# Who scales x by dt in a Mamba-2 block: ScalarE from PSUM, or GpSimd from SBUF

## The chip, the cores and the metric

The kernel runs on one core of a Trainium2 chip. The metric is the device time of one launch in microseconds, lower is better. The engines are named as the profile names them: PE (TensorE, matrix products), DVE (VectorE), ACT (ScalarE), POOL (GpSimd), SP (SyncE, which here only issues DMAs).

## The reference

Three blocks follow one another on x of 2 x 2048 tokens and 256 features: a routed feed-forward block, a Mamba-2 block, and the feed-forward block again.

```python
x = x + 0.5 * ffn(layernorm(x))
x = x + mamba2(layernorm(x))
x = x + 0.5 * ffn(layernorm(x))
```

Only the middle block changes. With 8 heads of 64 columns and a state of 64:

```python
z, xBC, dt = split(x @ W_in)
dt = softplus(dt + dt_bias)
xBC = silu(causal_conv4(xBC) + conv_b)        # gives x_ssm (512), B (64), C (64)
dA = exp(dt * A)
s = s * dA + (dt * x_ssm) outer B             # per token, per head
y = s . C + D * x_ssm
y = rmsnorm(y * silu(z)) * norm_weight
out = y @ W_out
```

## The kernel before

`mamba_block` cuts the 4096 tokens into 32 chunks of 128. Inside a chunk the recurrence is written as matrix products: `within(i)` (L1259) multiplies the masked decays `ex` by `xdt`, which is x times dt; `from_state(i)` (L1244) adds what the state before the chunk gives; `to_state(i)` (L1267) makes the new state from `xt`, which by then holds x times dt times the decay to the chunk's end.

Each engine has its own program, a loop over slots `s`, with a fixed order of steps in the slot and semaphore waits between engines. An engine never goes past a step that waits. Several chunks are in flight: in slot s chunk s is finished, chunk s+1 is prepared, chunks s+8 to s+10 are loaded and normalised. Four chunks share a group for the projection and the convolution, so the work of a slot also depends on s modulo 4 (tables `PROJECTED` and `TAPPED`, L835 and L836): blocks of 128 channels are projected in slots with remainder 3, 0 and 1, and convolved in slots with remainder 0, 1 and 2. Projection ends with group 7, so slots 27 to 31 have neither.

The steps round the change, for chunk s+1 unless said otherwise:

- PE `turn_xc` (L1297) transposes x into the PSUM bank `pT`. `turn_y(s)` (L1327) later writes the transposed y of chunk s into the same bank, so it must wait until x has been read from it.
- ACT `copy_x` (L1156) copies `pT` into `xt` in SBUF. Then ACT makes, in this order, `first_taps` of the first block of the slot where there is one, `decay(s+1, 1)` (four exponentials, L1171), `turn_x(s+9)` (L1126), `square(s)` (L1174), `copy_yT(s)` (L1178), `tanh` of convolved blocks and `first_taps` of a late block.
- POOL `scale_x` (L1062) makes three products of 128x512 from `xt`: `xdt` (L1068), `xD` (L1069) and, in place, `xt` (L1070). POOL's other steps in a slot are `decay_state`, `add_skip`, `gate_y`, `powers` and `add_tap`.
- PE after `turn_xc`: project the first block, `sums(s+1, 1)`, `turn_x(s+9)`, `turn_y(s)`, `project_z(s+2)`, project a late block, `turn_x2(s-2)`, and then, in the next slot, `from_state`, `project_dt` (which waits for DVE's `split_x`, L1491), `score`, `out_product`, `sums`, `within`, `to_state`.

The three waits that the change touches stand in these lines:

```python
pool.wait_ge(y_ready.sem, y_ready.done(i - 1))      # L1067, xdt is free again
pe.wait_ge(xdt_done.sem, xdt_done.done(i))          # L1260, within(i)
pe.wait_ge(xt_done.sem, xt_done.done(i + 1))        # L1330, turn_y(i)
```

Of the kernel before, what the change touches and what calls it, by code (L numbers as in the profile page):

```python
# [10 lines left out]
ALU = mybir.AluOpType  # L11
ACT = mybir.ActivationFunctionType
# [812 lines left out]
H = 8  # L825
HD = DIN // H
CONV = 4
NB = (DIN + 2 * NS) // P
GC = 4
# [11 lines left out]
def mamba_block(nc, c, keep, x, ys_d, w_in, conv_w, conv_b, dt_bias, a_log, d_skip, norm_w, w_out, x2, xn_d, batches):  # L841
# [6 lines left out]
    with ExitStack() as ctx:  # L848
# [5 lines left out]
        def step(name, unit=1):  # L854
# [25 lines left out]
        dts = sb("dts", [P, 3, NR, GC * H])  # L880
# [6 lines left out]
        xt, xdt, xD = (sb(n, [P, DIN]) for n in ("xt", "xdt", "xD"))  # L887
# [7 lines left out]
        DTR, DPOS, DABS, DU, DS, DS2, DQ, DT, DA, NCUM, ECUM, DEC, DECDT, ETOT = range(NR)  # L895

        pT, pP, small, pE, pY, pS, pZ, pO = (ctx.enter_context(nc.psum_tensor(f"bank{n}", [P, 512], F32)) for n in range(8))
# [13 lines left out]
        add1, add2, stats, aggr, stats2, aggr2, var_done, pow_done, nmr_done, norm_done, norm2_done = (  # L911
            step(n) for n in ("add1", "add2", "stats", "aggr", "stats2", "aggr2", "var", "pow", "nmr", "norm", "norm2"))
        xT_ready, xT_hi, xT_lo, z_ready, tz_done, sz_done, dt_ready, dt_added, x2T_ready, x2T_copied, logit_ready, logit_copied = (
            step(n) for n in ("xT", "xT_hi", "xT_lo", "z", "tz", "sz", "dt", "dt_added", "x2T", "x2T_copied", "logit", "logit_copied"))
        soft, exp_u, a_done, al_done, rest_done, cum_ready, cum_copied, exps, dec_in, dec_out, decdt, halo = (
            step(n) for n in ("soft", "exp_u", "a", "al", "rest", "cum", "cum_copied", "exps", "dec_in", "dec_out", "decdt", "halo"))
        p_ready, raw_done, tap0, tap_act, tap1, taps, tb_done, xc_done = (
            step(n) for n in ("p", "raw", "tap0", "tap_act", "tap1", "taps", "tb", "xc"))
# [4 lines left out]
        yT_ready, yT_copied, o_ready, xo_done = (step(n) for n in ("yT", "yT_copied", "o", "xo"))  # L923

        def row(G, n, k=0, chunks=GC):

            return dts[:, G % 3, n, k * H:(k + chunks) * H]

        def per_head(ap, width, parts=P):

            return ap.rearrange("p (h a) -> p h a", a=1).to_broadcast([parts, ap.shape[1], width])

        def by_head(ap, heads=H):
            return ap.rearrange("p (h d) -> p h d", h=heads)
# [4 lines left out]
        def live(i):  # L939
            return 0 <= i < T  # L940
# [75 lines left out]
        @block.gpsimd  # L1016
        def _(pool):
            chain = Chain(pool, consts)
            pool.memset(ident_bf[:, :], 0.0)
            pool.memset(future[:, :, :], 0.0)  # L1020
            pool.memset(S[:, :], 0.0)
            pool.memset(raw[:, :, 0:CONV - 1], 0.0)
            chain.link(pool.memset(pick[:, :], 0.0))
            for part in range(3):
                chain.link(pool.affine_select(out=pick[:, :], in_=pick[:, :], compare_op=ALU.not_equal, fill=1.0,
                                              base=-part * CH, pattern=[[-1, CH]], channel_multiplier=1))
            chain.link(pool.affine_select(out=ident_bf[:, :], in_=ident_bf[:, :], compare_op=ALU.not_equal, fill=1.0,
                                          base=0, pattern=[[-1, P]], channel_multiplier=1))
            chain.link(pool.affine_select(out=future[:, :, :], in_=future[:, :, :], compare_op=ALU.is_ge, fill=-1e30,
                                          base=0, pattern=[[0, GC], [1, P]], channel_multiplier=-1))  # L1030
            for s in (pow_done, xdt_done, xw_done, s1_done, td_done, yv_done, tap1):
                s.open(pool)

            def powers(s):

                q = s % 2
                pool.wait_ge(var_done.sem, var_done.done(at(s)))
                if live(s + 7):
                    pool.wait_ge(norm_done.sem, norm_done.done(s + 7))
                if live(s - 4):  # L1040
                    pool.wait_ge(norm2_done.sem, norm2_done.done(s - 4))
                if live(s - 3):
                    pool.wait_ge(xo_done.sem, xo_done.done(s - 3))
                pool.tensor_tensor(rstd[:, q, :], ve[:, q, :], c["neghalf"][:, 0:3], ALU.pow).then_inc(pow_done.sem, 1)  # L1044

            def decay_state(i):
                pool.wait_ge(S_done.sem, S_done.done(i - 1))
                pool.wait_ge(exps.sem, exps.done(i // GC))
                pool.wait_ge(i_ready.sem, i_ready.done(i))
                pool.tensor_tensor(by_head(S[:, :]), by_head(S[:, :]), per_head(dts[0:NS, i // GC % 3, ETOT, (i % GC) * H:(i % GC + 1) * H], HD, NS), ALU.mult).then_inc(s1_done.sem, 1)  # L1050

            def add_skip(i):
                pool.wait_ge(xw_done.sem, xw_done.done(i))
                pool.wait_ge(t1_done.sem, t1_done.done(i))
                pool.tensor_tensor(yv[:, :], yv[:, :], xD[:, :], ALU.add).then_inc(td_done.sem, 1)

            def gate_y(i):
                pool.wait_ge(sz_done.sem, sz_done.done(i))
                pool.wait_ge(t2_done.sem, t2_done.done(i))
                pool.tensor_tensor(yv[:, :], yv[:, :], sz[:, i % 2, :], ALU.mult).then_inc(yv_done.sem, 1)  # L1060

            def scale_x(i):  # L1062

                G, k = i // GC, i % GC
                pool.wait_ge(decdt.sem, decdt.done(G))
                pool.wait_ge(xt_done.sem, xt_done.done(i))
                pool.wait_ge(y_ready.sem, y_ready.done(i - 1))  # L1067
                pool.tensor_tensor(by_head(xdt[:, :]), by_head(xt[:, :]), per_head(row(G, DT, k, 1), HD), ALU.mult).then_inc(xdt_done.sem, 1)  # L1068
                pool.tensor_tensor(by_head(xD[:, :]), by_head(xt[:, :]), per_head(heads[:, 2, :], HD), ALU.mult)  # L1069
                pool.tensor_tensor(by_head(xt[:, :]), by_head(xt[:, :]), per_head(row(G, DECDT, k, 1), HD), ALU.mult).then_inc(xw_done.sem, 1)  # L1070

            def add_tap(G, m):
                b, j = ORDER[m], pooled(G, m)
                pool.wait_ge(tap_act.sem, tap_act.done(j))
                pool.tensor_tensor(acc[:, G % 2, b, :], acc[:, G % 2, b, :], tap[:, :], ALU.add).then_inc(tap1.sem, 1)  # L1075

            for s in SLOTS:
                if live(s):
                    if not ends(s):
                        decay_state(s)  # L1080
                    add_skip(s)
                    gate_y(s)
                if live(s + 1):
                    scale_x(s + 1)
                if rooted(s + 1):
                    powers(s + 1)
                for G, m in blocks(s, PROJECTED):
                    if m in BY_POOL:
                        add_tap(G, m)

        @block.scalar
        def _(act):
            for s in (al_done, norm_done, norm2_done, x2T_copied, logit_copied, xT_hi, tz_done, exp_u, exps, dec_out, raw_done, tap0, tap_act, tb_done,
                      xt_done, bt_done, ex0_done, ex_done, sq_done, yT_copied):
                s.open(act)
            act.dma_start(wst[:, :, :], w_in.rearrange("(k p) n -> p k n", p=P)).then_inc(in_loaded, 16)
            act.dma_start(wo[:, :, :], w_out.rearrange("(k p) n -> p k n", p=P)).then_inc(loads, 16)
# [58 lines left out]
            def copy_x(i):  # L1156
                act.wait_ge(turned.sem, turned.done(i))
                act.wait_ge(s_ready.sem, s_ready.done(i - 1))
                act.activation(xt[:, :], pT[:, :], ACT.Copy).then_inc(xt_done.sem, 1)

            def decay(i, half):

                G, k = i // GC, i % GC
                ready, done = ((e0_ready, ex0_done), (e1_ready, ex_done))[half]
                if half == 0:
                    act.wait_ge(cum_copied.sem, cum_copied.done(G))
                    act.wait_ge(y_ready.sem, y_ready.done(i - 2))
                act.wait_ge(ready.sem, ready.done(i))
                for n in range(GC):
                    h = half * GC + n  # L1170
                    last = act.activation(ex[:, i % 2, h, :], pE[:, n * P:(n + 1) * P], ACT.Exp, bias=dts[:, G % 3, NCUM, k * H + h:k * H + h + 1])  # L1171
                last.then_inc(done.sem, 1)
# [10 lines left out]
            for s in SLOTS:  # L1183
                first, late = blocks(s, PROJECTED)[:1], blocks(s, PROJECTED)[1:]
                G, G2 = cum_group(s), soft_group(s)
# [32 lines left out]
                    first_taps(*B)  # L1218
                if live(s + 1):
                    decay(s + 1, 1)  # L1220
                if live(s + 9):
                    turn_x(s + 9)
                if live(s):
# [8 lines left out]
        def _(pe):  # L1232
# [94 lines left out]
            def turn_y(i):  # L1327
                pe.wait_ge(yv_done.sem, yv_done.done(i))
                if live(i + 1):
                    pe.wait_ge(xt_done.sem, xt_done.done(i + 1))  # L1330
                for n in range(KI):
                    last = pe.transpose(pT[:, n * P:(n + 1) * P], yv[:, n * P:(n + 1) * P], ident[:, :])
                last.then_inc(yT_ready.sem, 1)
# [363 lines left out]
```

## Time and profile before

| | us |
|---|---|
| median of 3 runs | 1306.69 (1306.03 to 1313.96) |
| the profiled execution | 1312.65 |
| its span | 1310.9 |
| middle block within it, first to last `within` | 449.1 to 933.4 |
| mean granted PE clock over the span | 0.897 |

The profiled execution is 6 us above the median; all durations below are its own. Lines such as L1332 are lines of the program. A busy engine is one that executes; waits on semaphores are idle time. PEclk is the granted PE clock as a share of full speed. "PE bank L1332" is the group of instructions that line 1332 issues on PE with a PSUM bank as output.

### The profile page before, as it was taken

What the parts mean: (1) busy time and instruction counts of PE and PEld (TensorE: products, weight loads), DVE (VectorE), ACT (ScalarE), POOL (GpSimd) and SP (SyncE); (2) the same over time, 40 slices, a digit from 0 to 9 for tenths busy, and PEclk for the clock granted to TensorE, in tenths of its full rate; (3) what the DMA queues carried; (4) which work ended last, traced back from release to release, by engine and by line L of the source; (5) the groups of instructions that cost most, each with busy time, mean ns of one, the idle gap of its engine ahead of it and who ended that gap; (6) DMA issues with size and microseconds to landing.
All of it is one profiled execution on the core that took longest, in us unless ns stands there. A gap on an engine that the chain in (4) does not pass through costs nothing. (4 is left out here: it accounts for less than half of the span.)

```text
span 1310.9 us, 21923 instructions
## 1 busy us (share of the span) xinstructions
PE 1062.4 (81%) x6532; PEld 883.3 (67%) x6532; DVE 809.1 (62%) x1611; ACT 618.4 (47%) x1494; POOL 655.7 (50%) x593
## 2 busy tenths in 40 slices
PE   3747999999916788999999999989747999999900
PEld 3646999999914566766666666657536999999800
DVE  6974444444437898698989897875383444444434
ACT  1333555555513565556565656564333555555400
POOL 6913555555421465556565655567505555555300
PEclk9998999999966888788988888899868999999955
DMA  6861222222232111111111100000062222222178
GB/s 230 267 273 49 78 77 77 78 77 78 58 109 73 49 37 41 37 45 35 47 41 42 41 25 17 17 17 25 29 257 65 77 77 78 77 77 76 53 243 275
DMA packets 73242, 112.20 MB, mean 86 GB/s; under 512 B 10664, under 2 KB 60336, under 8 KB 71856
## 3 DMA queue, kind: packets, MB, share of 16 engines
q1 hardware_dynamic: 47888, 58.77, 13.2%
q0 software_dynamic: 13824, 37.77, 8.8%
q10 hardware_dynamic: 11424, 14.30, 3.2%
q8 instruction: 61, 1.00, 0.3%
q14 instruction: 45, 0.37, 0.1%
HBM read 66.76 MB, written 44.04 MB: 85 GB/s over the span
## 5 line engine op out<-in xcount | busy, mean ns | idle before, releaser
L399 POOL DMA_INDIRECT ys_d<-xs,row_of x144 | 142.0, 986 | 195.3 <-DVE xs L779 189.5
L768 DVE TENSOR_TENSOR xl<-pT,xh 128x256 fp32r<-128x256 f32 x144 | 61.1, 424 | 223.9 <-ACT xh L476 223.9
L394 POOL DMA_INDIRECT xs<-xn_d,token_of x144 | 139.8, 971 | 114.4 <-DVE token_of L753 71.2
L463 ACT ACTIVATE hs<-pH 128x512 f32<-128x512 f32 x144 | 86.0, 597 | 233.8 <-PE pH L581 233.8
L773 DVE TENSOR_TENSOR h2l<-hs,h2h 128x512 fp32r<-128x512 f32 x144 | 99.8, 693 | 78.0 <-ACT h2h L471 77.8
L1548 DVE SCALAR_TENSOR_TENSOR acc<-raw,cwh,acc 128x512 f32<-128x512 f32 x104 | 120.9, 1208 | 2.2 <-POOL acc L1075 1.2
L1171 ACT ACTIVATE ex<-bank,dts 128x128 f32<-128x128 f32 x256 | 72.5, 366 | 98.9 <-PE bank L1316 98.9
L601 PE MATMUL pY<-w2h,h2h 128*128 x576 | 102.8, 300 | 0.5 <-DVE h2l L773 0.3
L1060 POOL TENSOR_TENSOR yv<-yv,sz 128x512 f32<-128x512 f32 x32 | 48.0, 1501 | 95.8 <-DVE yv L1598 95.8
L581 PE MATMUL pH<-w1h,xh 128*128 x288 | 92.7, 404 | 1.8 <-DVE xl L768 1.1
L581 PE MATMUL pH<-w1l,xh 128*128 x288 | 92.7, 404 | 0.0
L1241 PE MATMUL bank<-wo,yT 128*128 128x256 f32 x256 | 92.5, 525 | 0.0
L601 PE MATMUL pY<-w2h,h2l 128*128 x576 | 92.1, 282 | 0.0
L581 PE MATMUL pH<-w1h,xl 128*128 x288 | 90.7, 397 | 0.0
L601 PE MATMUL pY<-w2l,h2h 128*128 x576 | 90.5, 279 | 0.0
L471 ACT ACTIVATE h2h<-pR 128x512 fp32r<-128x512 f32 x144 | 88.8, 616 | 0.0
L469 ACT ACTIVATE hs<-pR 128x512 f32<-128x512 f32 x144 | 87.4, 607 | 1.5 <-PE pR L590 1.5
L590 PE MATMUL pR<-ident,hs 128*128 128x128 f32 x576 | 86.5, 273 | 0.0
L1044 POOL TENSOR_TENSOR m_rstd<-m_ve,neghalf 128x3 f32<-128x3 f32 x43 | 40.9, 952 | 88.5 <-DVE m_ve L1474 88.5
L601 PEld LDWEIGHTS pY<-w2h,h2h 128*128 128x128 f32 x576 | 77.6, 189 | 1.6 <-issue 1.5
L601 PEld LDWEIGHTS pY<-w2h,h2l 128*128 128x128 f32 x576 | 78.1, 188 | 0.0
L601 PEld LDWEIGHTS pY<-w2l,h2h 128*128 128x128 f32 x576 | 77.8, 188 | 0.0
(248 smaller groups left out, 2668.8 us busy)
## 6 DMA issues: line engine op xcount, KB each, us to landing
m_yg<-ys_d SPq DMA_DIRECT2D x64, 128.0 KB, 2.1
xs<-ys_d SPq DMA_DIRECT2D x16, 512.0 KB, 6.0
wst<-in_L_ffn_w_dram ACTq DMA_DIRECT2D x8, 512.0 KB, 4.7
xs<-in_L_attn_x_dram SPq DMA_DIRECT2D x8, 512.0 KB, 6.6
hs<-in_L_ffn_w_dram ACTq DMA_DIRECT2D x8, 512.0 KB, 5.0
xn_d<-xs SPq DMA_DIRECT2D x8, 512.0 KB, 3.2
lo_d<-w1l SPq DMA_DIRECT2D x1, 4096.0 KB, 11.8
lo_d<-w2l SPq DMA_DIRECT2D x1, 4096.0 KB, 21.3
```

The lines of the kernel that those rows point to most:

```text
L394: pool.indirect_dma_start(out=xg[:, t % NX, :], out_offset=None, in_=xn_d, in_offset=bass.IndirectOffsetOnAxis(ap=token_of[:, t:t + 1], ax ...
L399: pool.indirect_dma_start(out=ys_d, out_offset=bass.IndirectOffsetOnAxis(ap=row_of[:, t:t + 1], axis=0), in_=y[:, t % NX, :], in_offset=No ...
L463: act.activation(r[:, u, :], pH[u][:, :], ACT.Relu).then_inc(relu_done.sem, 1)
L469: act.activation(h2[:, u, :, :], turned_h, ACT.Square)
L471: act.activation(h2h[:, u, :, :], turned_h, ACT.Square).then_inc(sq_done.sem, 1)
L581: last = pe.matmul(pH[u][:, :], a[:, u, k, :], w[:, k * HID:(k + 1) * HID], start=(n == 0), stop=(n == 3 * KD - 1))
L590: last = pe.transpose(pR[u][:, k * P:(k + 1) * P], r[:, u, k * P:(k + 1) * P], ident[:, :])
L601: last = pe.matmul(pY[u][:, 0:D], a[:, u, k, :], w[:, k * D:(k + 1) * D], start=(n == 0), stop=(n == 3 * KH - 1))
L773: dve.tensor_tensor(h2l[:, u, :, :], h2[:, u, :, :], h2h[:, u, :, :].bitcast(F32), ALU.subtract).then_inc(h2_split.sem, 1)
L1171: last = act.activation(ex[:, i % 2, h, :], pE[:, n * P:(n + 1) * P], ACT.Exp, bias=dts[:, G % 3, NCUM, k * H + h:k * H + h + 1])
L1241: last = pe.matmul(out, a, b, start=(m == 0), stop=(m == len(parts) - 1))
L1548: ins = dve.scalar_tensor_tensor(a, raw[:, b, n:n + GT], cwh[:, b, n:n + 1], a, ALU.mult, ALU.add)
```

## The change

POOL no longer makes `xdt`. ACT makes it in a new step `scale_x`, right behind `decay(s+1, 1)`: eight ACTIVATEs of 128x64, each reading one head's columns from `pT` and scaling them by the head's dt, given as a column of `dts`. PE's `turn_y(s)`, which overwrites `pT`, now waits for `xdt` of chunk s+1 in place of `xt`. POOL keeps `xD` and the in-place product of `xt`.

```diff
-            for s in (pow_done, xdt_done, xw_done, s1_done, td_done, yv_done, tap1):
+            for s in (pow_done, xw_done, s1_done, td_done, yv_done, tap1):
                 s.open(pool)
@@ POOL scale_x
                 pool.wait_ge(xt_done.sem, xt_done.done(i))
-                pool.wait_ge(y_ready.sem, y_ready.done(i - 1))
-                pool.tensor_tensor(by_head(xdt[:, :]), by_head(xt[:, :]), per_head(row(G, DT, k, 1), HD), ALU.mult).then_inc(xdt_done.sem, 1)
                 pool.tensor_tensor(by_head(xD[:, :]), by_head(xt[:, :]), per_head(heads[:, 2, :], HD), ALU.mult)
@@ ACT
                 act.activation(xt[:, :], pT[:, :], ACT.Copy).then_inc(xt_done.sem, 1)
+
+            def scale_x(i):
+                act.wait_ge(a_done.sem, a_done.done(i // GC))
+                act.wait_ge(y_ready.sem, y_ready.done(i - 1))
+                for h in range(H):
+                    col = i % GC * H + h
+                    last = act.activation(xdt[:, h * HD:(h + 1) * HD], pT[:, h * HD:(h + 1) * HD], ACT.Copy, scale=dts[:, i // GC % 3, DT, col:col + 1])
+                last.then_inc(xdt_done.sem, 1)
@@ ACT, the slot
                     decay(s + 1, 1)
+                    scale_x(s + 1)
                 if live(s + 9):
                     turn_x(s + 9)
@@ PE turn_y
                 if live(i + 1):
-                    pe.wait_ge(xt_done.sem, xt_done.done(i + 1))
+                    pe.wait_ge(xdt_done.sem, xdt_done.done(i + 1))
```

## Rows read from the trace of the kernel before

**Rows 1.** The page, part 2: granted clock in 40 slices of the span.

```profile
PEclk9998999999966888788988888899868999999955
```

**Rows 2.** Windows: us, busy us (x instructions) of PE, PEld, DVE, ACT, POOL; PEclk, DMA.

```profile
634.00:700.00 66.00, 59.83 (x314) 44.19 (x315) 57.94 (x105) 37.78 (x100) 36.99 (x30) 0.89 0.13 41
...
895.00:927.00 32.00, 30.99 (x183) 22.40 (x183) 18.64 (x30) 17.20 (x52) 25.26 (x21) 1.00 0.08 26
```

**Rows 3.** Waits of PE from 500 to 872: us in total, times, longest.

```profile
PE bank L1241 <- DVE xTl L1491: 19.8, 9, 2.3
```

**Rows 4.** Timeline of slot 11: start, us, engine, line, operation, count [idle before <-releaser].

```profile
637.90 0.60 ACT L1159 ACTIVATE xt<-bank 128x512 f32<-128x512 f32 x1 [0.25 <-PE bank L1301]
...
638.63 1.04 POOL L1068 TENSOR_TENSOR xdt<-xt,dts 128x512 f32<-128x512 f32 x1
...
639.76 0.60 PE L1332 MATMUL bank<-ident,yv 128*128 128x128 f32 x4
...
640.63 1.12 ACT L1171 ACTIVATE ex<-bank,dts 128x128 f32<-128x128 f32 x4
...
643.88 0.41 PE L1358 MATMUL bank<-ident,m_xn 128*128 128x128 f32 x2 [0.73 <-issue]
...
645.04 1.12 PE L1246 MATMUL bank<-S,CT 64*128 64x512 f32 x2
...
648.81 1.89 PE L1264 MATMUL bank<-xdt,ex 128*128 128x64 f32 x16
```

**Rows 5.** Timeline, the same two steps in slots 1 and 25.

```profile
474.26 0.66 PE L1332 MATMUL bank<-ident,yv 128*128 128x128 f32 x4 [0.21 <-POOL yv L1060]
...
474.77 1.12 ACT L1171 ACTIVATE ex<-bank,dts 128x128 f32<-128x128 f32 x4
...
865.53 0.60 PE L1332 MATMUL bank<-ident,yv 128*128 128x128 f32 x4
...
866.62 1.12 ACT L1171 ACTIVATE ex<-bank,dts 128x128 f32<-128x128 f32 x4
```

**Rows 6.** Timeline of slot 12 (remainder 0), and PE's next idle.

```profile
654.68 0.60 PE L1332 MATMUL bank<-ident,yv 128*128 128x128 f32 x4
...
656.17 1.12 ACT L1171 ACTIVATE ex<-bank,dts 128x128 f32<-128x128 f32 x4
...
660.65 0.39 PE L1241 MATMUL bank<-wih,xTh 128*128 128x8 f32 x2 [2.07 <-DVE xTl L1491]
```

**Rows 7.** Timeline of slot 14 (remainder 2), and PE's next idle.

```profile
687.21 1.13 ACT L1171 ACTIVATE ex<-bank,dts 128x128 f32<-128x128 f32 x4
...
687.46 0.63 PE L1332 MATMUL bank<-ident,yv 128*128 128x128 f32 x4
...
693.06 0.59 PE L1241 MATMUL bank<-wih,xTh 128*128 128x8 f32 x2 [2.31 <-DVE xTl L1491]
```

**Rows 8.** Timeline of slot 27, the first of the last four full ones.

```profile
894.55 0.60 ACT L1159 ACTIVATE xt<-bank 128x512 f32<-128x512 f32 x1 [0.25 <-PE bank L1301]
...
895.04 1.14 ACT L1171 ACTIVATE ex<-bank,dts 128x128 f32<-128x128 f32 x4
...
895.29 0.63 PE L1332 MATMUL bank<-ident,yv 128*128 128x128 f32 x4 [0.34 <-ACT xt L1159]
```

**Rows 9.** ACT instructions by line: ns min/median/max, first and last start, form.

```profile
L1171 ACT ACTIVATE ex<-bank,dts x256: 341/367/389, 438.1 to 927.8; 128x128 f32<-128x128 f32 x128
...
L1124 ACT ACTIVATE logits<-bank x32: 177/177/178, 495.4 to 948.1; 128x8 f32<-128x8 f32 x32
...
L1159 ACT ACTIVATE xt<-bank x32: 578/597/602, 441.1 to 926.5; 128x512 f32<-128x512 f32 x32
```

**Rows 10.** Timeline: the same eight matmuls in slots 12 and 15.

```profile
646.56 1.97 PE L1241 MATMUL bank<-wo,yT 128*128 128x256 f32 x8
...
695.21 3.76 PE L1241 MATMUL bank<-wo,yT 128*128 128x256 f32 x8
```

**Rows 11.** DVE's convolution taps by line: ns min/median/max.

```profile
L1548 DVE SCALAR_TENSOR_TENSOR acc<-raw,cwh,acc x104: 718/1421/1846, 416.7 to 883.5; 128x512 f32<-128x512 f32 x104
```

More of the change, by code:

```diff
@@ L1093, in _ @@
             for s in (al_done, norm_done, norm2_done, x2T_copied, logit_copied, xT_hi, tz_done, exp_u, exps, dec_out, raw_done, tap0, tap_act, tb_done,
-                      xt_done, bt_done, ex0_done, ex_done, sq_done, yT_copied):
+                      xt_done, xdt_done, bt_done, ex0_done, ex_done, sq_done, yT_copied):
                 s.open(act)
```

## The prediction, made before the changed kernel ran

> **What bounds the kernel now.** I read the page first, and in it the row of the granted clock: its dip to 0.6 in the 12th and 13th slice is where the first feed-forward block gives way to the middle one [rows 1]. Only the middle block changes, so everything outside it keeps its time. Next come the windows. Four slots, 66 us, hold 59.8 us of PE work, 57.9 of DVE, 37.8 of ACT and 37.0 of POOL [rows 2]. PE is busy nine tenths, and near the end of the block, where nothing is projected or convolved, 31.0 of 32 us. POOL, which the change relieves, and ACT, which it loads, both have room as averages. That settles little: what counts is which step waits for which. PE's waits from 500 to 872 us come first of all to 19.8 us for DVE's `split_x` [rows 3], and none is for `xdt`. So the product that POOL makes today is on nobody's path: it is ready at 638.63 + 1.04 = 639.67 while `within` uses it at 648.81 [rows 4]. The timeline of single slots then shows what the change ties together.
>
> **The product removed from POOL.** 32 products of 1.04 to 1.5 us leave POOL. What waited behind them are POOL's own `xD` and `xt`, needed by PE only in the next slot, as `xdt` was. I cost this edit at nothing. What hides POOL's work is PE's own queue, which is nowhere waiting for these three.
>
> **The eight copies on ACT.** The trace has no 128x64 copy with a scale column. The nearest row is the exponential of 128x128 from PSUM with a bias column: 0.367 us alone, and four in a row take 1.12 us [rows 4, 9]. So one starts (1.12 - 0.367) / 3 = 0.251 us after the other, 0.116 us before the other's end. A column costs (597 - 177) / 504 = 0.833 ns, from the copies of 512 and of 8 columns [rows 9]. 64 columns fewer are 0.053 us: 0.314 us alone, 0.198 apart. Eight take 7 x 0.198 + 0.314 = 1.70 us, and since the first starts 0.116 us before the last exponential's end, `xdt` is done 1.58 us after that end. The lower bound is the eight-column copy, eight times 0.177 less 0.116, or 1.30 us; the upper is eight times the exponential alone, 2.94 us less 0.116, or 2.82. I take 1.58, since source, engine and pointer operand are those of the exponential and only the width differs.
>
> The Trainium skill, "ScalarE: Activation LUTs", section "What ACT_TABLE_LOAD costs", gives 186 ns plus 0.833 ns a column, 93 ns for each pointer operand, and 93 ns of overlap between neighbours. By it a copy is 332 ns and the eight take 2.01 us, 1.91 behind the exponentials, and the total below would be some 10 us higher. The trace agrees on the cost of a column, but its exponentials follow one another at 0.251 us where the skill gives 0.294, so I keep the row.
>
> **The new wait of `turn_y`.** This is where the time goes. Today `turn_y` needs only `copy_x`, which ends at 638.50 in slot 11, and starts at 639.76 without idling. The copies stand in ACT's order behind the second half of `decay`, which in slot 11 runs from 640.63 to 641.75 because ACT has taken the first projected block in between [rows 4]. With 1.58 us for the copies and 0.14 us from an ACT end to the PE start it releases (895.15 to 895.29 [rows 8]), `turn_y` can start 1.72 us after `decay` ends. The delay D is that moment less today's start.
>
> Behind `turn_y` in PE's queue stand `project_z`, the late projection, `turn_x2`, and the next slot's `from_state`, on which DVE's `scale_state` and so the rest of that slot wait. On ACT, `turn_x`, `square` and `copy_yT` come 1.6 us later, `copy_yT` by all of D. D is then lost, less the idle that PE has today between `turn_y` and the next thing that it waits for from a chain that D does not move.
>
> *Remainders 1 and 3.* Slot 11: 641.75 + 1.72 - 639.76 = 3.71 us. The idle of 0.73 us behind it, ahead of L1358 [rows 4], is a wait for ACT's copy of the late block, and that block is itself projected behind `turn_y`; it moves along and gives nothing back. There are 13 such slots (1, 3, 5 to 25), with D from 3.35 in slot 1 to 3.93 in slot 25 [rows 5]. 13 x 3.7 = 48 us.
>
> *Remainder 0.* Slot 12: 657.29 + 1.72 - 654.68 = 4.33 us, but PE idles 2.07 us afterwards for `split_x`, which ends DVE's convolution taps and does not depend on `turn_y` [rows 6]. 2.26 us are left, in seven slots (0 to 24): 16 us.
>
> *Remainder 2.* Slot 14: 688.34 + 1.72 - 687.46 = 2.60 us against 2.31 us of idle [rows 7]. 0.3 us are left, in six slots (2 to 22): 2 us; in slot 26 nothing.
>
> *Slots 27 to 30.* 896.18 + 1.72 - 895.29 = 2.61 us with PE otherwise busy throughout [rows 2, 8]: 4 x 2.61 = 10 us. In slot 31 there is no chunk 32 to wait for.
>
> Together 48 + 16 + 2 + 10 = 76 us.
>
> **The clock.** Half clock stretches PE's work: the eight `out_product` matmuls take 1.97 us at full clock and 3.76 at half, 1.8 us more [rows 10]. The 66 us at a mean of 0.89 hold 66 x 0.11 x 2 = 14.5 us at half clock in four slots, about 3.6 us in each, while 895 to 927 has none [rows 2]. Row 693.06 shows such a stretch behind an idle PE of 2.3 us [rows 7, 10]. With a stall of about 2.6 to 4.3 us in every slot I expect each slot to have its stretch, as most have now; new ones are those of slots 27 to 30, 4 x 1.8 = 7 us. Bounds: none of the 7, or a second stretch in each of 30 slots, 54 us.
>
> **The sum.** 76 + 7 = 83 us. The profiled execution of 1312.65 would become 1396. It stands 6 us over the median, and that difference has nothing to do with the change, so on the median: 1306.7 + 83 = 1390 us. The lower bound of the copies takes 0.28 us from each of the 24 counted slots outside remainder 2 and all 2 us of those with it: -9. The upper bound adds 1.24 x 30 = 37. So the forecast's own range is 1306.7 + 76 - 9 = 1374 to about 1425, the upper end leaving part of the two high bounds to the rival below.
>
> **The rivals.**
>
> *Rival 1: the low clock falls into the stall.* Granted clock sinks some time behind an idle stretch. If it sinks while PE stands before `turn_y` and is back when it starts, the stretches that cost 1.8 us each today cost nothing. One in each of slots 3 to 26 is 24 x 1.8 = 43 us back: 1306.7 + 76 - 43 = 1340. For it: the stall, up to 4.3 us, is about as long as a stretch. Against it: at 693.06 the clock was low after the idle, on work [rows 7, 10]. Chance 0.13.
>
> *Rival 2: a second low stretch in the slots,* or copies at their upper bound: 1306.7 + 76 + 54 = 1437, or 1306.7 + 83 + 37 = 1427. Chance 0.08.
>
> *Rival 3: faster, by what POOL gives back to DVE.* A tap takes 0.718 us at best and 1.421 at the median [rows 11], and POOL runs beside it. If the slow taps are slowed by POOL, one product less, 1.04 to 1.5 us long, returns half of its time, 0.7 us in each of 32 slots: 22 us, or 1306.7 - 22 = 1285, where DVE sets the pace. This decides only if D is below the idle behind `turn_y`: D would have to fall under 2.3 us in remainder 2 and to zero in remainders 1 and 3. With the copies at their lower bound D in slot 11 is still 3.4 us. Chance 0.03.
>
> The Trainium skill, "SBUF — State Buffer", section "SBUF: two separate sides", says that VectorE and GpSimd hold a shared pair of SBUF ports as an exclusive lock, so that the loser is blocked for the whole instruction. By that rule the gain of rival 3 on DVE is real, and the spread of the taps agrees; it would shorten the taps and leave the stall of `turn_y` untouched.
>
> *Rival 4: no change.* `turn_y` waits, but what is behind it on PE turns out to have slack that the idle rows hide, as where PE waits 19.8 us for `split_x` [rows 3]. It needs 76 us of slack, and the block has 66 - 59.8 = 6.2 us of idle PE in four slots [rows 2], some 50 us in all, of which 2.07 + 2.31 us in four slots are already taken off. Chance 0.04.
>
> **How the numbers follow.** The forecast, 1374 to 1425, has 0.72. From 1340 up, rival 1 comes in, around that value. The range 1345 to 1425 leaves out about half of rival 1 and all of the other three, some 2 in 10. Under 1% either way, 13 us, is what a measurement of this kernel can't tell from no change. Faster by over 1%: rival 3, 0.03. Within 1%: rival 4, 0.04. Slower: forecast and rivals 1 and 2, 0.72 + 0.13 + 0.08 = 0.93. The predicted time is 1390.
>
> **What would show it.** In the profile after: a PE wait at `turn_y` for ACT's `xdt` in 31 slots, 2 to 4 us each, 80 us or more in total; `xdt` on ACT at 0.31 us an instruction and 1.7 us for the eight; PE's wait for `split_x` in remainders 0 and 2 gone or small; the four slots from 27 on 2.6 us or more longer each; POOL's busy time 33 us less or more; `within` still not waiting for `xdt`. The prediction is wrong if `turn_y` waits much less than D, or if it does and the block is still no longer, which would mean that the time comes back behind it.

## The result

| | median, us | ratio to before, 95% interval |
|---|---|---|
| before | 1308.2 | |
| changed | 1435.8 | 1.097 (1.094 to 1.100) |
| forecast | 1390, range 1345 to 1425 | |

The change costs 127.6 us, 9.7%. The direction and the place were forecast; the size was not: 83 us were expected, and the time lies above the range.

The page of the changed kernel, its first parts (busy us of each engine, share of the span, instructions; then the granted clock in 40 slices, which answers to [rows 1]) and its costliest group that waits:

```profile
span 1432.6 us, 22179 instructions
...
PE 1111.5 (78%) x6532; PEld 916.7 (64%) x6532; DVE 788.3 (55%) x1611; ACT 673.2 (47%) x1750; POOL 605.6 (42%) x561
...
PEclk9998999999667898878898978797756999999965
...
L1339 PE MATMUL bank<-ident,yv 128*128 128x128 f32 x128 | 30.9, 388 | 111.5 <-ACT xdt L1164 109.2
```

The same parts of the page of the kernel before:

```profile
span 1310.9 us, 21923 instructions
...
PE 1062.4 (81%) x6532; PEld 883.3 (67%) x6532; DVE 809.1 (62%) x1611; ACT 618.4 (47%) x1494; POOL 655.7 (50%) x593
```

PE issues the same 6532 matmuls in both. The span grew by 121.7 us, and it splits into two parts. PE's idle time, span less busy, went from 248.5 to 321.1 us: 72.6 more. PE's busy time went from 1062.4 to 1111.5 us: 49.1 more for the same instructions. The first is the stall, the second the clock: the same matmuls, more of them at the lower clock. PE waited 109.2 us at `turn_y` (now L1339) for ACT's `xdt`, in 31 slots; before, its largest wait in the block was the one for `split_x` [rows 3]. That one, 22.1 us from 449 to 933, is gone from the block, and other waits with it; so idle grew by less than 109 us.

Windows over the middle block, before (449 to 933) and changed (449 to 1053); columns as in [rows 2]:

```profile
449.00:933.00 484.00, 436.93 (x2306) 323.26 (x2305) 401.20 (x699) 274.03 (x730) 292.11 (x231) 0.90 0.11 33
```

```profile
449.00:1053.00 604.00, 484.13 (x2299) 355.04 (x2299) 378.41 (x701) 327.06 (x974) 241.12 (x199) 0.83 0.09 27
```

Mean clocks of 0.90 and 0.83 are 484 x 0.10 x 2 = 97 us and 604 x 0.17 x 2 = 205 us at half clock. By the two windows the block lost 47 us of matmul time (484.1 less 436.9) on 108 more microseconds at half clock, 0.44 us for each.

The timeline of slot 27 shows both parts; it answers to [rows 8]:

```profile
986.09 1.14 ACT L1177 ACTIVATE ex<-bank,dts 128x128 f32<-128x128 f32 x4
...
987.09 1.78 ACT L1164 ACTIVATE xdt<-bank,dts 128x64 f32<-128x64 f32 x8
...
989.00 1.08 PE L1339 MATMUL bank<-ident,yv 128*128 128x128 f32 x4 [3.01 <-ACT xdt L1164]
...
995.88 3.76 PE L1248 MATMUL bank<-wo,yT 128*128 128x256 f32 x8
```

And its windows:

```profile
984.00:987.00 3.00, 2.00 (x14) 1.11 (x12) 0.97 (x2) 1.74 (x6) 1.94 (x2) 1.00 0.12 44
987.00:989.00 2.00, 0.00 (x0) 0.03 (x1) 0.00 (x0) 2.00 (x10) 1.37 (x2) 0.66 0.01 4
989.00:1001.00 12.00, 11.99 (x35) 8.48 (x36) 3.80 (x8) 2.51 (x8) 4.03 (x3) 0.50 0.01 1
```

The eight copies take 1.78 us and PE starts 1.77 us after the exponentials' end at 987.23 (1.72 forecast). PE stands for 3.01 us. The clock sinks to half, 1.2 GHz, during the stall, and stays there for the next 12 us while PE is busy all the time. The eight `out_product` matmuls take 3.76 us, as at half clock in [rows 10]. In the kernel before this part of the block ran at 1.00 [rows 2].

Slot 27 is one of the long cases. Windows from one `turn_y` to the next show how the half clock is spread over the slots. Here is slot 11 of the kernel before:

```profile
639.76:654.68 14.92, 14.19 (x84) 10.45 (x82) 14.07 (x32) 9.72 (x28) 7.31 (x7) 1.00 0.14 46
```

And slots 10 and 14 of the changed kernel:

```profile
657.29:679.67 22.38, 18.76 (x75) 13.51 (x76) 16.12 (x37) 10.82 (x34) 6.44 (x6) 0.71 0.10 30
738.58:755.37 16.79, 13.17 (x74) 10.38 (x74) 14.15 (x37) 10.68 (x34) 5.54 (x5) 0.90 0.14 42
```

Before, 12 of the 31 slots from 0 to 30 had no half clock at all: nine of the 13 with remainder 1 or 3, such as slot 11, and slots 27 to 29. In the changed kernel every slot has some: 3 to 7 us in 21 of them, and 10 to 14 us in ten (0, 7, 8, 10, 19, 20, 22, 27, 29 and 30). The ten are not those with the longest stalls. In slots 10 and 14 PE stands for the same 2.79 us ahead of `turn_y`, and 13 us at half clock follow in one, 3.4 us in the other; in slots 27 and 28 it is 3.01 us, with 12.3 and 4.8 us. What decides between a short and a long stretch no run here shows.

### The profile page after: what moved, and what is told of

Its sections match the earlier page's. It is cut to its first block and busy times, and to the rows that moved or that the text cites. A ratio compares the mean times of both kernels' runs of the same rounds, so it can differ in the third digit from the quotient of the medians.

```text
span 1432.6 us, 22179 instructions
## 1 busy us (share of the span) xinstructions
PE 1111.5 (78%) x6532; PEld 916.7 (64%) x6532; DVE 788.3 (55%) x1611; ACT 673.2 (47%) x1750; POOL 605.6 (42%) x561
## 5 line engine op out<-in xcount | busy, mean ns | idle before, releaser
L1339 PE MATMUL bank<-ident,yv 128*128 128x128 f32 x128 | 30.9, 388 | 111.5 <-ACT xdt L1164 109.2
L1177 ACT ACTIVATE ex<-bank,dts 128x128 f32<-128x128 f32 x256 | 72.6, 366 | 92.7 <-PE bank L1323 92.7
L1555 DVE SCALAR_TENSOR_TENSOR acc<-raw,cwh,acc 128x512 f32<-128x512 f32 x104 | 111.6, 1119 | 2.2 <-POOL acc L1073 1.2
L1060 POOL TENSOR_TENSOR yv<-yv,sz 128x512 f32<-128x512 f32 x32 | 42.9, 1341 | 129.7 <-DVE yv L1605 129.7
L1339 PEld LDWEIGHTS bank<-ident,yv 128*128 128x128 f32 x128 | 19.7, 190 | 118.9 <-issue 116.5
L1248 PE MATMUL bank<-wo,yT 128*128 128x256 f32 x256 | 86.3, 496 | 0.0
## 6 DMA issues: line engine op xcount, KB each, us to landing
lo_d<-w1l SPq DMA_DIRECT2D x1, 4096.0 KB, 11.8
```

The lines of the kernel that those rows point to most:

```text
L1248: last = pe.matmul(out, a, b, start=(m == 0), stop=(m == len(parts) - 1))
L1555: ins = dve.scalar_tensor_tensor(a, raw[:, b, n:n + GT], cwh[:, b, n:n + 1], a, ALU.mult, ALU.add)
```

## The experiments

Two ideas had to be told apart. Theory T: the stall costs what the delays add up to, some 76 us, and the rest is matmuls at half clock that the stall brings on. Rival R: the rest is a longer chain through ACT and DVE, which the half clock only accompanies. All ratios are to the kernel before, run on the same chip.

### Keeping PE busy in the stall

```diff
             def turn_y(i):
                 pe.wait_ge(yv_done.sem, yv_done.done(i))
+                for _ in range(12 if live(i + 1) else 0):
+                    pe.matmul(pY[:, :], ident_bf[:, :], future[...], start=True, stop=True)
                 if live(i + 1):
                     pe.wait_ge(xdt_done.sem, xdt_done.done(i + 1))
```

> The changed kernel, with twelve extra matmuls of 128x512 bf16 on PE ahead of the wait of turn_y for xdt, behind its wait for yv, into a bank that is free there. Their results are overwritten. At full clock they take about 2.6 us, less than the shortest wait of 2.79 us. Theory T (of the 127 us lost, some 73 are PE standing at turn_y and some 49 are PE's own matmuls at half clock, brought on by that standing): the granted clock stays near full, PE's real matmuls lose their 49 us, and the time falls to 1385 to 1400 us. Rival R (the loss beyond the stall is a longer chain through ACT and DVE, and the half clock only accompanies it): the time stays within 10 us of 1436 or grows, whatever the clock does.

Measured: 1350.3 us, ratio 1.032 (1.028 to 1.037), 85 us below the changed kernel. Parts of its page, its group of extra matmuls, and its window over the block:

```profile
span 1347.8 us, 22892 instructions
...
PE 1109.0 (82%) x6904; PEld 890.3 (66%) x6904; DVE 794.8 (59%) x1611; ACT 670.7 (50%) x1750; POOL 614.9 (46%) x561
...
L1337 PE MATMUL bank<-future,ident_bf 128*128 128x512 bf16 x372 | 85.4, 379 | 2.1 <-POOL yv L1060 2.0
...
449.00:969.00 520.00, 480.92 (x2662) 327.89 (x2661) 386.07 (x699) 326.16 (x980) 251.63 (x199) 0.98 0.10 31
```

The clock in the block is 0.98. PE's own matmuls, 1109.0 less the 85.4 of the extra ones, take 1023.6 us: 88 less than in the changed kernel, and 39 less than in the kernel before, which pays for half clock too. Work that computes nothing made the changed kernel 6% faster. R is refuted. T had the mechanism and too small a number, since I had expected only the added half clock to go, and the old went as well.

With half as many, six:

> As the first filled version of the changed kernel, but six extra matmuls in place of twelve ahead of the wait of turn_y, some 1.4 us, so that 1.4 to 2.9 us of idle are left there. Theory T (an idle stretch of about 3 us and more brings the long half-clock stretches): idle at turn_y falls from 109 to some 66 us, half clock from 209 us to under 120, and the time is 1360 to 1395 us. Rival (only a filled stall helps): above 1420 us.

Measured: 1379.4 us, ratio 1.052 (1.049 to 1.056). Its span is 1387.7, PE 1111.3 busy, of which the 186 extra matmuls are 45.2; it waits 64.4 us for `xdt`, and the clock in the block (449 to 1008) is 0.90, as in the kernel before, or 559 x 0.10 x 2 = 112 us at half clock. All three lie where T put them. That a stall has to be about 3 us long for this is not shown: slot 10 above has its 13 us behind a stall of 2.79.

The control has the twelve on the other side of the wait:

```diff
                 if live(i + 1):
                     pe.wait_ge(xdt_done.sem, xdt_done.done(i + 1))
+                for _ in range(12 if live(i + 1) else 0):
+                    pe.matmul(pY[:, :], ident_bf[:, :], future[...], start=True, stop=True)
```

> The changed kernel with the same twelve matmuls behind turn_y's wait for xdt in place of ahead of it: the same work on PE, but the idle stretch stays. A control. Theory T (filling the idle stretch is what helps): the stall and the half clock stay, and 31 x 2.75 us of work come on top where PE has no slack, so 1480 to 1560 us. Rival (extra matmuls keep the clock up wherever they stand): below 1436 us.

Measured: 1484.0 us, ratio 1.131 (1.128 to 1.135), at the low end of what T gave. From its page and its groups:

```profile
span 1484.4 us, 22923 instructions
...
PE 1162.1 (78%) x6904; PEld 907.7 (61%) x6904; DVE 775.7 (52%) x1611; ACT 673.2 (45%) x1750; POOL 614.7 (41%) x561
...
L1339 PE MATMUL bank<-future,ident_bf 128*128 128x512 bf16 x372 | 138.5, 549 | 109.2 <-ACT xdt L1164 109.2
```

The stall stays at 109.2 us, as expected. The half clock did not stay, as I had expected it to, on the kernel's own matmuls: these take 1162.1 - 138.5 = 1023.6 us here too. A part of the extra ones ran at the low clock in their place: the 372 are busy for 138.5 us against 85.4, 549 ns each on average against 379 (neighbours overlap, so the busy time is less than the sum). So both halves of the rival are answered: extra matmuls do help the clock behind the wait, but there their own time is on PE's path. The mean clock from 449 to 1105 is 0.89, or 656 x 0.11 x 2 = 144 us at half clock, against 205 in the changed kernel with the same 109.2 us of stall. So the stall by itself does not fix the time at half clock; the work that PE finds behind it counts too.

These profiles give the split for each kernel. Idle here is span less busy, with the extra matmuls counted to it, less the 248.5 us of before; clock is the kernel's own busy PE time less 1062.4:

| kernel | idle or extra matmuls, us | clock, us | sum = span less 1310.9 |
|---|---|---|---|
| changed | +72.6 | +49.1 | +121.7 |
| 6 ahead of the wait | +73.1 | +3.7 | +76.8 |
| 12 ahead of the wait | +75.7 | -38.8 | +36.9 |
| 12 behind the wait | +212.3, of which 138.5 extra | -38.8 | +173.5 |

Whatever the clock does, the stall costs 73 to 76 us (in the last row 212.3 - 138.5 = 73.8). That is the 76 us of the prediction.

### The stall without copies, and with one copy

The kernel before, with one wait more:

```diff
                 if live(i + 1):
                     pe.wait_ge(xt_done.sem, xt_done.done(i + 1))
+                    pe.wait_ge(ex_done.sem, ex_done.done(i + 1))
```

> The kernel before, POOL's product and all, with one more wait: turn_y(s) also waits for the second half of the exponentials of chunk s+1. This is the position in ACT's order alone, without any copy. Theory T: turn_y waits about 2.1 us in remainders 1 and 3, 2.7 in remainder 0 with 2.1 hidden, 1.0 in remainder 2, hidden, and 1.0 in slots 27 to 30, together 36 us, plus what the clock adds, up to 20: 1335 to 1365 us. Rival R' (only a stall as long as the copies make it matters): below 1325 us.

Measured: 1340.6 us, ratio 1.026 (1.018 to 1.034). PE waits 57.0 us at `turn_y`, 2.8 at the longest, and its page reads:

```profile
PE 1062.5 (79%) x6532; PEld 880.0 (66%) x6532; DVE 804.6 (60%) x1611; ACT 620.5 (46%) x1494; POOL 653.0 (49%) x593
```

Its span is 1342.3. Idle grew by 31.3 us against 36 added up, and the busy time by 0.1: in this execution these shorter stalls cost the idle that they add, and no clock. (The four runs spread widely, from 1336 to 1356 us.)

One copy in the place of eight:

```diff
-                for h in range(H):
+                for h in range(1):
                     col = i % GC * H + h
-                    last = act.activation(xdt[:, h * HD:(h + 1) * HD], pT[:, h * HD:(h + 1) * HD], ...)
+                    last = act.activation(xdt[:, :], pT[:, :], ...)
```

> The changed kernel with one copy of 128x512 in place of the eight of 128x64; all heads are scaled by the dt of the first, so the scaling per head is left out. The copy takes about 0.7 us in place of 1.78. Theory T: the wait of turn_y shrinks by about 1.1 us in each of 31 slots, some 30 us where it was not hidden, and the clock gives back part of its 49 us: 1375 to 1400 us. Rival R' (the number of ACT instructions hardly matters, the wait for decay does): 1420 us or more.

Measured: 1377.9 us, ratio 1.055 (1.049 to 1.061), inside what T gave. The copy takes 0.705 us, PE waits 76.3 us at `turn_y`, 3.4 at the longest, idle grew by 42.4 us and busy by 17.7 (1080.1 us in a span of 1371.0). This lies between the two others: the clock's part is 0 for 57 us of waits, 18 for 76, and 49 for 109. It does not grow in proportion with the stall, and the next kernel shows that the total of the waits does not fix it either.

### The same copies in other places of ACT's order

First with `turn_y` freed of them, by reading `xt` in SBUF:

```diff
@@ ACT scale_x
+                act.wait_ge(xt_done.sem, xt_done.done(i))
...
-                    last = act.activation(xdt[...], pT[:, h * HD:(h + 1) * HD], ACT.Copy, scale=...)
+                    last = act.activation(xdt[...], xt[:, h * HD:(h + 1) * HD], ACT.Copy, scale=...)
@@ POOL scale_x, ahead of the in-place product of xt
+                pool.wait_ge(xdt_done.sem, xdt_done.done(i))
@@ PE turn_y
-                    pe.wait_ge(xdt_done.sem, xdt_done.done(i + 1))
+                    pe.wait_ge(xt_done.sem, xt_done.done(i + 1))
```

> The changed kernel, but ACT's eight copies read xt in SBUF, turn_y waits for xt only as before, and POOL waits for xdt ahead of its in-place product of xt. ACT does the same eight copies in the same place. Theory T (the wait of turn_y for the copies is what costs): most of the loss goes, 1306 to 1325 us, ACT's later turn_x, square and copy_yT costing at most 1.8 us in the slots where PE or DVE wait for them. Rival R (eight copies in ACT's order lengthen ACT's chain, wherever x is read from): 1380 us or more.

Measured: 1376.9 us, ratio 1.051 (1.047 to 1.055). T missed this one by 50 us. PE's waits over the block (us in total, times, longest):

```profile
PE bank L1367 <- issue: 32.4, 12, 3.0
PE bank L1250 <- DVE xTl L1500: 21.2, 12, 2.2
PE bank L1250 <- ACT m_xT L1119: 11.7, 9, 3.9
```

`turn_y` no longer waits for the copies, but `turn_x2` (L1367) does: 32.4 us, against 8.8 in the changed kernel. It needs the late block's copy out of PSUM, and on ACT that copy stands behind the eight, `square` and `copy_yT`. In the changed kernel this second route is hidden: the late block is itself projected after the stall. With the first wait gone it comes to light. Its page has a span of 1376.7 and PE 1103.6 us busy: idle +24.6, clock +41.2 us, with the clock in the block at 0.83. So most of this kernel's loss is half clock, and with a third of the added idle it has nearly the clock's part of the changed kernel (24.6 and 41.2 us against 72.6 and 49.1). Two things differ from the changed kernel besides the wait: read from SBUF, the eight copies take 2.02 us (554.35 to 556.37 in one slot) in place of 1.78, and POOL's in-place product now waits for them; what these two cost was not measured apart.

Then as ACT's last step of the slot, behind the late block:

```diff
                     decay(s + 1, 1)
-                    scale_x(s + 1)
@@ the end of ACT's slot
                 for B in late:
                     first_taps(*B)
+                if live(s + 1):
+                    scale_x(s + 1)
```

> The copies from SBUF, with scale_x as ACT's last step of the slot, behind the late block's copy and taps; turn_y waits for xt only; POOL's in-place product of xt waits for xdt, and powers stands behind that. Nothing of ACT's that PE needs in the slot is later than before; copy_x2T and tanh_z of the next slot are up to 1.8 us later. Theory T2: waits of turn_x2 for the late block return to 0.7 us, and the time is 1306 to 1335 us. Rival R (ACT with 1.8 us more in a slot is slower wherever the copies stand): 1365 us or more.

Measured: 1373.3 us, ratio 1.047 (1.042 to 1.051). The wait of `turn_x2` did fall, to 10.9 us, but T2's time, at most 1335 us, was wrong, and R's, 1365 or more, came out. What is late now stands at the head of the next slot:

```profile
PE bank L1251 <- ACT m_xT L1119: 36.5, 25, 3.9
```

`copy_x2T` comes behind the copies, and `score` and everything after it on PE wait for it. `turn_y` also waits longer for POOL's `yv`, 13.0 us in the block against 5.0 before. R as it was stated, slower wherever the copies stand, is tested by the next run.

Last, as early as it can be, straight behind `copy_x`:

```diff
                     copy_x(s + 1)
+                    scale_x(s + 1)
                 for B in first:
                     first_taps(*B)
                 if live(s + 1):
                     decay(s + 1, 1)
-                    scale_x(s + 1)
```

> The changed kernel with ACT's scale_x right behind copy_x, ahead of the first block's taps and of decay. Theory T1 (it is the wait of turn_y that costs): xdt is ready about 0.5 us after turn_y could start, so its waits shrink to some 15 to 20 us in all, and the time is 1320 to 1340 us. Theory T2 (any 1.8 us of ACT ahead of the copy of the late block costs, as with the copies from SBUF, by that copy, turn_x2 behind it and the clock): 1360 to 1385 us.

Measured: 1323.6 us, ratio 1.010 (1.006 to 1.015): of the 9.7% of the change 1% is left. The timeline of one slot:

```profile
645.49 0.60 ACT L1157 ACTIVATE xt<-bank 128x512 f32<-128x512 f32 x1 [0.26 <-PE bank L1308]
645.99 1.75 ACT L1164 ACTIVATE xdt<-bank,dts 128x64 f32<-128x64 f32 x8
...
647.56 0.67 ACT L1136 ACTIVATE raw<-bank 128x512 f32<-128x512 f32 x1
...
647.88 0.63 PE L1339 MATMUL bank<-ident,yv 128*128 128x128 f32 x4 [0.36 <-ACT xdt L1164]
```

The copies run while PE projects the first block, in part of which ACT used to wait for that block. `turn_y` waits 0.36 us here and 33.1 us over the block, and the clock is 0.90 as before. T1's time is right, though it had put these waits at 15 to 20 us, and T2, that 1.8 us of ACT anywhere ahead of the late block must cost 50 us or more, is wrong. Of R of the kernel before this one, slower wherever the copies stand, 1% is left, far from its 1365 us.

### The product alone, and the half clock that was there before

POOL's product left out, with nothing in its place; `xdt` is a constant, so the scaling of x by dt within a chunk is missing:

```diff
-                pool.tensor_tensor(by_head(xdt[:, :]), by_head(xt[:, :]), per_head(row(G, DT, k, 1), HD), ALU.mult).then_inc(xdt_done.sem, 1)
-                pool.tensor_tensor(by_head(xD[:, :]), by_head(xt[:, :]), per_head(heads[:, 2, :], HD), ALU.mult)
+                pool.tensor_tensor(by_head(xD[:, :]), by_head(xt[:, :]), per_head(heads[:, 2, :], HD), ALU.mult).then_inc(xdt_done.sem, 1)
```

> The kernel before without POOL's product for xdt, which stays at a constant; the scaling of x by dt within a chunk is left out. Nothing takes its place. Theory T (the product is on nobody's path): within 8 us of before, 1300 to 1315 us. Rival 3 of the prediction (POOL's product slows DVE's taps and that is on the path): 1285 us.

Measured: 1305.8 us, ratio 0.996 (0.993 to 0.999), some 5 us. Taking the product from POOL and doing it nowhere brings 0.4%, at most 0.7% by the interval. DVE did get faster, as the third rival had it; its taps in this kernel (ns min/median/max) against a median of 1421 [rows 11]:

```profile
L1548 DVE SCALAR_TENSOR_TENSOR acc<-raw,cwh,acc x104: 719/896/1845, 416.4 to 875.4; 128x512 f32<-128x512 f32 x104
```

The median overstates it. All 104 together are busy for 112.1 us against 120.9, 1123 ns on average against 1208: 9 us, where the rival had 22. How much of the 9 us was on the path can't be told from a gain of 5.

The kernel before with PE kept busy where it idles:

```diff
             for s in SLOTS:
+                if live(s + 8) and s % GC in (1, 3):
+                    keep_busy(8)                  # 128x512 bf16 matmuls into pY
                 if live(s + 8) and s % GC != 0:
                     project_dt(s + 8, s)
+                if s in (25, 27):
+                    keep_busy(8)
                 if live(s - 3):
                     score(s - 3, s)
...
+                if late and live(s - 2):
+                    keep_busy(3)
                 if live(s - 2):
                     turn_x2(s - 2, s)
```

> The kernel before, with extra matmuls of 128x512 bf16 in the places where PE idles: eight ahead of project_dt in slots of remainder 1 and 3, three ahead of turn_x2 where a late block was projected, eight ahead of score in slots 25 and 27. They take 0.23 us each and should fit in the idle of 2.1 to 2.3, 0.7 to 1.1 and 2.4 to 2.8 us. Theory T (half clock is paid in full, and the kernel before pays for some 95 us of it in the middle block): most of that goes, real matmuls lose 30 to 45 us and the time falls to 1265 to 1285 us. The pure stall of the change is then the filled changed kernel less this one, 1350 less some 1275, and should be the 76 us of the delays added up. Rival R (half clock mostly falls where another engine sets the pace): 1300 us or more.

Measured: 1291.9 us, ratio 0.984 (0.981 to 0.987). It beats both kernels. The clock in the block rose from 0.90 to 0.96:

```profile
449.00:928.00 479.00, 443.65 (x2450) 315.74 (x2485) 412.25 (x710) 279.00 (x737) 295.04 (x234) 0.96 0.11 35
```

It missed the expected 1265 to 1285 and stayed below the rival's 1300. The expected difference to the filled changed kernel, 76 us, came out as 1350.3 - 1291.9 = 58, or 64 by the two ratios, 1.0325 and 0.9839, since the two ran on different chips. Why was not settled: a part of the fills may lie on PE's path, but this profile lacks some PE records, and the split into idle and busy can't be made from it.

Early copies and fills together, with four fills ahead of `turn_y` as well:

> The changed kernel with scale_x right behind copy_x, with the fills of the filled kernel before, and four fills (0.9 us) ahead of turn_y's wait. Theory T: the copies early cost 10 to 15 us by themselves and the fills give back 15 to 25: 1290 to 1310 us, about the filled kernel before and below both kernels. Rival (the two don't add): 1320 us or more.

Measured: 1315.4 us, ratio 1.004 (1.002 to 1.005). This is 8 us better than the early copies alone and not below before; it lies between T's 1290 to 1310 and the rival's 1320. The clock is 0.97, but the 304 fills take 79.8 us of PE, where with early copies alone it had waited 33.1 us at `turn_y` and 11.8 at `turn_x2`. By the split of the table (span 1310.0, PE 1094.4 us busy), PE's own matmuls take 47.8 us less than before, and idle and fills together 46.9 us more. The two cancel: what a fill takes beyond the idle that it stands in is itself on the path.

## Why the prediction missed

*The removal from POOL, costed at nothing.* Right: 0.4%. (POOL's busy time fell by 50 us, of which the product was 37.9; the products that stayed ran shorter.)

*The eight copies.* Right as a sum. 1.70 us forecast, 1.78 measured; one copy is 0.359 us at the median against 0.314, and they start closer together for their length than I took; `turn_y` starts 1.77 us after the exponentials' end, against 1.72. The Trainium skill's formula ("ScalarE: Activation LUTs", section "What ACT_TABLE_LOAD costs") gave 0.332 alone and 2.01 for the eight: nearer for one, farther for the row, since the copies follow one another at (1.78 - 0.359) / 7 = 0.203 us, where it has 0.239.

*The stall.* Right, slot by slot: PE stands for 3.6 us with remainder 1 and 3 (3.8 in slots 23 and 25; 3.7 forecast), 4.2 with remainder 0 (4.5 in slot 24; 4.33 forecast), 2.8 to 3.0 with remainder 2 (2.60) and 3.0 in slots 27 to 30 (2.61 beyond an idle of 0.34 that was there). 76 us were added up from D less the idle behind it; the split gives 72.6 for the changed kernel and 73 to 76 for three others that share the wait.

*The clock.* This is the step that failed. It stood at 7 us, with a bound of 54, and measured 49.1 us. I spread the 14.5 us at half clock of four slots evenly, 3.6 us in each, took this for a fixed size, and asked only in which slots there would be new ones; I named slots 27 to 30. Both halves of that were wrong. Nine more slots, those of remainder 1 and 3 named above, had none either and got one. And the size changed: ten slots now have 10 to 14 us, as slot 27, where half clock held for the stall's end and 12 us of work behind it. In the block, 97 us at half clock became 205. 76 + 49 = 125 us, and the measured difference is 127.6 (121.7 between the profiled spans).

*The rivals.* Rival 1, half clock falling into the stall for free, had the wrong sign: the windows of slot 27 show it beginning there and reaching 12 us beyond. Rival 2, more half clock, is what happened: 1437 us forecast with a chance of 0.08, 1435.8 measured. It had too small a chance, and the range, which stopped at 1425, left it out. That its number is right to 1 us is partly luck: it priced a second stretch of 1.8 us in each of 30 slots, and what came was a first one in twelve slots and a long one in ten. Rival 3 is right that the taps get shorter, but by 9 us in all and not 22. Rival 4 fell with the stall.

*What I had not seen at all.* The copies' place in ACT's order has a second cost, by the late block's copy, which costs nothing as long as `turn_y` waits longer, and shows when that wait is removed.

## What to carry to other kernels

A wait put into PE's queue, where PE sets the pace, can cost twice: its length less the idle behind it, and the matmuls that then run at half clock. Here the second was two thirds of the first in the changed kernel and nothing for the shorter waits of the kernel without copies, so it has to be priced with its own upper bound. Count it from the clock of each slot, not from a mean over several. An engine with room by its average is no cheap place by that alone; the gaps in its order are: the same eight copies cost 9.7% and, moved into a gap, 1.0%; read from SBUF they cost 5.1% in the first place and 4.7% at the slot's end. Before a wait is given up as unavoidable, look at what PE could do in it.

## What the runs showed of the hardware

Matmuls that compute nothing, put into PE's idle stretch, raised the mean granted clock of the block from 0.83 to 0.98 and saved 85 us of 1436; put behind the same stretch, they left the kernel's own matmuls at the same 1023.6 us of busy time and ran slow themselves, 549 ns on average in place of 379. Over three kernels the clock's part grew faster than the stall, 0, 18 and 49 us for 57, 76 and 109 us of waits at `turn_y`; but it is no function of the wait alone, since the kernel with copies from SBUF has 41 us of it with 24.6 us more idle, and two stalls of 2.79 us in one kernel were followed by 13 and by 3.4 us at half clock. Half clock can last through 12 us in which PE is busy without a break (slot 27). And DVE's 104 taps of 128x512 went from 1208 ns on average to 1123 ns, their median from 1421 to 896, when one of POOL's products, 128x512 as well, was gone.
